# Inverse roots of the scan stage on GpSimd as a power, ScalarE's silus in halves, and two sums around Ln set apart

## What is computed

```python
h = x * rsqrt(mean(x * x, -1) + 1e-5) * norm_scale          # first inverse root, per token
xs, res = split(h @ w_in, 2, -1)
res = silu(res)                                             # the gate
xs = silu(causal_depthwise_conv(xs, conv_w, conv_b))
delta, B, C = split(xs @ w_xproj, [16, 32], -1)
delta = softplus(delta @ w_dt + b_dt)
deltaA = exp(delta[..., None] * -exp(A_log))
deltaBx = (delta * xs)[..., None] * B[:, :, None, :]
ys = scan(h_t = deltaA_t * h_(t-1) + deltaBx_t)             # along the tokens
x2 = layernorm(x + (x + ((sum_n ys * C) + xs * D) * res @ w_out))   # eps 1e-5
n = x2 * rsqrt(mean(x2 * x2, -1) + 1e-8) * norm_weight      # router and experts read n
# sigmoid router, top 2 of 8 experts, expert FFNs 256 -> 1024 -> 256 with relu,
# a shared FFN of the same size, and a last layer norm over x2 + both
```

## Time and profile before

| | |
|---|---|
| median of 3 runs | 1816.91 us (1810.32 to 1822.06) |
| profiled execution, span | 1813.2 us |
| PE busy | 1512.9 us, 83% |
| DVE busy | 1268.1 us, 70% |
| ACT busy | 947.0 us, 52% |
| POOL busy | 888.3 us, 49% |
| the chain that ended last | PE 49%, DVE 30%, ACT 11%, issue 7%, DMA 2% |

### The profile page before, as it was taken

One profiled execution on the slowest core, in us unless ns is written; L12 is line 12 of the kernel. 1 busy time (PEld: TensorE's weight loads), 2 busy tenths in 40 slices (PEclk: granted clock), 3 DMA queues, 4 the chain that ended last, 5 costly groups with the idle time before them and its releaser, 6 DMA issues.

```text
span 1813.2 us, 24484 instructions
## 1 busy us (share of the span) xinstructions
PE 1512.9 (83%) x6945; PEld 968.6 (53%) x6946; DVE 1268.1 (70%) x2203; ACT 947.0 (52%) x1802; POOL 888.3 (49%) x412
## 2 busy tenths in 40 slices
PE   7485789887898997898897857896999999999980
PEld 3121225424434533444443513575999999999970
DVE  3488999999999899999999999622333333333327
ACT  4577666668657568557568644221333333333324
POOL 0676776696685786685786794110111111111114
PEclk9698997898897898897898988988999999999995
DMA  5833653452541642632632641555555555555538
GB/s 153 213 88 76 147 121 74 120 144 61 135 130 48 160 115 67 157 109 55 163 99 65 163 122 24 181 175 198 177 184 188 174 178 189 184 174 177 188 114 271
DMA packets 136951, 252.14 MB, mean 139 GB/s; under 512 B 15313, under 2 KB 68418, under 8 KB 136754
## 3 DMA queue, kind: packets, MB, share of 16 engines
q1 hardware_dynamic: 130402, 233.49, 45.8%
q0 software_dynamic: 6480, 17.83, 2.7%
HBM read 205.76 MB, written 45.51 MB: 139 GB/s over the span
## 4 chain that ended last, share of the span: by engine, by line
PE 49%; DVE 30%; ACT 11%; issue 7%; DMA 2%; SPq 1%; POOL 0%; DVEq 0%; ACTq 0%; POOLq 0%
DVE psH L1041 17%; PE psP L1553 14%; PE psH L1542 14%; DVE big L1050 6%; PE psP L1383 5%; PE psP L1372 4%; PE psA L1481 3%; PE psA L1462 2%; PE psP L1446 2%; PE psP L1401 2%; ACT psH L885 2%; ACT L885 1%; PE psA L1472 1%; PE psP L1530 1%; DMA xb<-rows_dram 1%
## 5 line engine op out<-in xcount | busy, mean ns | idle before, releaser
L467 POOL TENSOR_TENSOR big<-big,B 128x2048 f32<-128x2048 f32 x128 | 578.3, 4528 | 216.3 <-PE psA L1481 140.4
L885 ACT ACTIVATE psH<-big,A_q 128x512 f32<-128x512 f32 x512 | 352.1, 691 | 181.7 <-DVE big L1050 173.3
L1041 DVE TENSOR_TENSOR_SCAN psH<-psH,big 128x512 f32<-128x512 f32 x256 | 312.2, 1220 | 57.3 <-ACT psH L885 37.9
L1050 DVE TENSOR_TENSOR big<-psH,C 128x512 f32<-128x512 f32 x512 | 345.7, 675 | 0.0
L1041 DVE TENSOR_TENSOR_SCAN psH<-psH,carry,big 128x512 f32<-128x512 f32 x256 | 328.4, 1283 | 17.0 <-ACT psH L885 17.0
L508 POOL DMA_INDIRECT con_dram<-eo,dest x71 | 67.8, 955 | 481.2 <-ACT eo L945 473.3
L1481 PE MATMUL psA<-big,gsum 128*32 128x512 f32 x1024 | 236.9, 674 | 64.8 <-DVE big L1050 64.6
L1542 PEld LDWEIGHTS psH<-nTb,ew_s 128*128 128x128 f32 x2272 | 266.1, 193 | 3.6
L1542 PE MATMUL psH<-nTb,ew_s 128*128 128x128 f32 x2272 | 266.3, 276 | 0.0
L1553 PE MATMUL psP<-big,hT 128*128 x1136 | 258.7, 381 | 1.0 <-DVE eb L1291 0.7
L1553 PEld LDWEIGHTS psP<-big,hT 128*128 128x128 f32 x1136 | 211.4, 191 | 27.9 <-issue 1.8
(11 more groups left out here) (180 smaller groups left out, 1593.0 us busy)
## 6 DMA issues: line engine op xcount, KB each, us to landing
ew_s<-in_L_ffn_ew_dram SPq DMA_DIRECT2D x71, 1024.0 KB, 4.9
big<-ud_dram SPq DMA_DIRECT2D x128, 512.0 KB, 8.5
ud_dram<-ud SPq DMA_DIRECT2D x32, 512.0 KB, 2.6
xb<-rows_dram SPq DMA_DIRECT2D x71, 130.0 KB, 2.1
B<-bc_dram SPq DMA_DIRECT2D x128, 64.0 KB, 5.4
C<-bc_dram SPq DMA_DIRECT2D x128, 64.0 KB, 8.5
big<-in_L_ffn_ew_dram SPq DMA_DIRECT2D x8, 1024.0 KB, 12.0
big<-con_dram SPq DMA_DIRECT2D x16, 512.0 KB, 8.8
```

What stands on the lines that cost most here:

```text
L467: nc.gpsimd.tensor_tensor(X[:, Q % NX], rep[:, g % 2, 1], B4[:, f:f + 1, :].broadcast_to([P, NR, TC]), ALU.mult).then_inc(bx_ready, 1)
L885: nc.scalar.activation(psH[:, r, :], rep[:, g % 2, 0, r, :], ACT.Exp, scale=A_q[:, c, r, f:f + 1]).then_inc(dA_ready, 1)
L1041: nc.vector.tensor_tensor_scan(psH[:, r, :], psH[:, r, :], X[:, Q % NX, r, :], start, ALU.mult, ALU.add).then_inc(scan_done, 1)
L1050: nc.vector.tensor_tensor(X[:, Q % NX, r, :], psH[:, r, :], C4[:, f, :], ALU.mult).then_inc(hc_ready, 1)
```

## The change

- The inverse roots are made by POOL as a power with exponent −0.5: two instructions at the start (of 4 and 28 columns) for the first norm, and for each tile a function `roots` of five small instructions behind its `input_step` of step 7 (the last tile's at the end of the stage). ACT's Sqrt and DVE's reciprocals, `inverses` and `biases` are gone. DVE's `add_rows` waits for POOL's result.
- `silu_xs` and `silu_gate` are cut in halves of 1024 columns: xs at (6, 3) and (8, 1) for the next tile, the gate at (3, 2) and (12, 1) of its own tile.
- Of the softplus, `dt_exp` moves from (2, 0) to (1, 3) and from (11, 0) to (10, 3), and 1 + x is made ahead of Ln, at (2, 0) and (11, 0). The subtraction of 1 behind it moves from (11, 3) to (11, 2).
- `read_rows` moves from (2, 0) and (2, 1) to (2, 2) and (3, 0), and one `read_in` from (6, 3) to (7, 0).
- In the start, Exp of A_log is taken earlier.

ACT loads a table 64 times before and 96 times after.

```diff
@@ POOL
+            def roots(k):
+
+                pool.wait_ge(v_ready, k + 1)
+                link.done(nc.gpsimd.tensor_tensor(spread[:, 2], spread[:, 0],
+                                                  less_half[:, 0:2 * NSUB].rearrange("p (a s) -> p a s", a=2),
+                                                  ALU.pow)).wait()
+                link.done(nc.gpsimd.tensor_tensor(nbias[:, 0], mv[:, :, 0], spread[:, 2, 0], ALU.mult))
+                link.done(nc.gpsimd.tensor_tensor(spread[:, 1, 0], spread[:, 0, 0], spread[:, 2, 0], ALU.mult)).wait()
+                nc.gpsimd.tensor_scalar(nbias[:, 0], nbias[:, 0], -1.0, None, ALU.mult).then_inc(nb_ready, 1)
+                nc.gpsimd.tensor_tensor(nbias[:, 1], spread[:, 1, 0], spread[:, 2, 1], ALU.mult).then_inc(n1_ready, 1)
...
+            nc.gpsimd.memset(less_half[:], -0.5).then_inc(s_half, 1)
+            pool.wait_ge(s_half, 1)
+            pool.wait_ge(s_ms, 1)
+            nc.gpsimd.tensor_tensor(rstd1[:, 0:NSUB], rstd1[:, 0:NSUB], less_half[:, 0:NSUB],
+                                    ALU.pow).then_inc(s_rstd, 1)
...
+                    if k >= 1 and q == 7:
+                        roots(k - 1)
...
                     nc.gpsimd.memset(zero[:], 0.0).then_inc(s_base, 1)
+                    roots(NT - 1)
@@ ACT
-            act.wait_ge(s_ms, 1)
-            nc.scalar.activation(rstd1[:, 0:NSUB], rstd1[:, 0:NSUB], ACT.Sqrt).then_inc(s_root, 1)
...
-            def silu_xs(k):
-                evacuated(act, k, ("C", CH - 2), ("C", CH - 1))
-                nc.scalar.activation(xs[:, k % 2], xs[:, k % 2], ACT.Silu).then_inc(xs_ready, 1)
...
+            def silu_xs(k, h):
+                evacuated(act, k, ("C", 2 * h), ("C", 2 * h + 1))
+                part = xs[:, k % 2, 2 * h:2 * h + 2]
+                nc.scalar.activation(part, part, ACT.Silu).then_inc(xs_ready, 1)
...
-                         (2, 0): [(read_rows, 1, 0), (dt_exp, 0, 1)], (2, 1): [(read_rows, 1, 1), (dt_ln, 0, 1)],
-                         (2, 2): [(dt_one_plus, 0, 1)], (2, 3): [(dt_less_one, 0, 1)],
+                         (1, 3): [(dt_exp, 0, 1)], (2, 0): [(dt_one_plus, 0, 1)],
+                         (2, 1): [(dt_ln, 0, 1)], (2, 2): [(read_rows, 1, 0)], (2, 3): [(dt_less_one, 0, 1)],
+                         (3, 0): [(read_rows, 1, 1)], (3, 2): [(silu_gate, 0, 0)],
...
-                         (6, 1): [(read_conv, 1, 1)], (6, 2): [(read_in, 1, 3)], (6, 3): [(read_in, 1, 6)],
...
-                         (8, 0): [(read_conv, 1, 3)], (8, 1): [(root, -1), (silu_xs, 1), (silu_gate, 1)],
+                         (6, 1): [(read_conv, 1, 1)], (6, 2): [(read_in, 1, 3)], (6, 3): [(silu_xs, 1, 0)],
+                         (7, 0): [(read_in, 1, 6)], (7, 1): [(read_conv, 1, 2)], (7, 2): [(read_in, 1, 7)],
+                         (8, 0): [(read_conv, 1, 3)], (8, 1): [(silu_xs, 1, 1)],
...
+                         (12, 0): [(relu_up, -1, 1)], (12, 1): [(silu_gate, 0, 1)], (13, 0): [(relu_up, -1, 2)], (13, 2): [(relu_up, -1, 3)],
@@ DVE
-            def inverses(k):
-                dve.wait_ge(sq_ready, k + 1)
-                link.done(nc.vector.reciprocal(spread[:, 2], spread[:, 1]))
...
             def add_rows(k, h, i):
                 s = 2 * h + i
                 dve.wait_ge(o_done, k * UPS + (h + 1) * PER_HALF)
-                link.wait()
+                dve.wait_ge(n1_ready, k + 1)
...
-                         (8, 0): [(inverses, -1), (biases, -1)],
```

More of the change, by code:

```diff
@@ L797, in dt_ln @@
                     after(act, ud_out[j], 16 * (2 * k + h))
+                nc.scalar.activation(ud[:, :, 0], spe[:], ACT.Copy, bias=1.0).then_inc(sp_act, 1)
+            def dt_ln(k, h):
                 nc.scalar.activation(ud[:, :, 1], spe[:], ACT.Ln, bias=1.0).then_inc(sp_act, 1)
[L800 to L801 removed]
             def dt_less_one(k, h):
[L804 removed]
+                act.wait_ge(sp_act, 6 * (2 * k + h) + 4)
                 nc.scalar.activation(ud[:, :, 0], ud[:, :, 0], ACT.Copy, bias=-1.0).then_inc(sp_act, 1)
@@ L809, in dt_in @@
                 dt_relu(k, c)
-            def root(k):
-                act.wait_ge(v_ready, k + 1)
-                nc.scalar.activation(spread[:, 1], spread[:, 0], ACT.Sqrt).then_inc(sq_ready, 1)
             def normalize(k, i):
@@ L889, in _ @@
                 read_rows(0, d)
+            act.wait_ge(s_A, 16 * NG)
+            nc.scalar.activation(A_q[:], A_q[:], ACT.Exp).then_inc(s_neg, 1)
             read_in(0, 0)
@@ L896, in _ @@
                 evacuated(act, 0, ("C", c))
-                nc.scalar.activation(xs[:, 0, c], xs[:, 0, c], ACT.Silu).then_inc(s_xs0 if c < CH - 1 else xs_ready, 1)
-            act.wait_ge(s_A, 16 * NG)
-            nc.scalar.activation(A_q[:], A_q[:], ACT.Exp).then_inc(s_root, 1)
+                nc.scalar.activation(xs[:, 0, c], xs[:, 0, c], ACT.Silu).then_inc(s_xs0 if c % 2 == 0 else xs_ready, 1)
             read_proj(0)
@@ L913, in _ @@
             nc.scalar.activation(ud[:, 1, 0], ud[:, 1, 0], ACT.Copy, bias=-1.0).then_inc(sp_act, 1)
-            act.wait_ge(s_ms, 2)
-            nc.scalar.activation(rstd1[:, NSUB:], rstd1[:, NSUB:], ACT.Sqrt).then_inc(s_root, 1)
             act.wait_ge(rwT_full, 1)
@@ L1027, in _ @@
             dve.wait_ge(s_u0, 3)
-            dve.wait_ge(xs_ready, 1)
+            dve.wait_ge(s_xs0, 1)
             nc.vector.tensor_tensor(ud[:, 0, 1], ud[:, 0, 0], xs[:, 0, 0], ALU.mult).then_inc(u_ready, 1)
-            dve.wait_ge(s_root, 3)
-            nc.vector.reciprocal(later, later).then_inc(s_rstd, 1)
             def scan(k, q, r):
```

56 lines of the change are left out of this document (26 added, 30 removed).

## The result

The changed kernel takes 1862.99 us in the median of 4 runs (1859.27 to 1867.14), against 1818.82 for the kernel before; the ratio is 1.024, with a 95% interval of 1.0205 to 1.0274. It is slower by 44 us. The forecast was slower at 1850, with a range of 1815 to 1868. The profiled execution spans 1857.5 us, 44.3 more than before.

The account below looks back on a forecast made before the run. The scan stage was taken as bound by DVE's work plus its waits. The terms, −19 + 17 + 8 + 12 + 15 + 0 = +33 us on 1813.2, gave 1846, or 1850 as a median; range 1815 to 1868.

Parts of the forecast that it names:

- A: Step 8: the root leaves ACT and DVE and the silus are halved, so the decay ends earlier; −19 us.
- B: Steps 2 and 3: late T bank reads delay PE's output product, so DVE waits at its residual; +17 us.
- C: Step 12: the gate's second half comes between two decays; +2.0 us in even tiles, +0.7 in odd, +8 in all.
- D: Step 4: one of DVE's small variance instructions falls into a POOL multiplication of 4.5 us; +12 us (0 to 17).
- E: Step 14: DVE's chain of eight can wait for POOL's first two next-tile multiplications; +15 us, 27 at most.
- F: The ends: a 1.28 us load before the first scan, tile 0 −2, tile 7 and tail +1; sum 0.
- G: POOL's power at step 7: taken as 0.5 us, with 10.8 us of room covering all five instructions.
- Rival 1: Port waits between DVE and POOL don't deepen, D and E about 0: 1820 to 1823 us; chance 0.25.
- Rival 2: POOL's multiplications miss the chain at step 14, whose waits go, −12 us: 1811 as a median; chance 0.08.
- Rival 3: The power is dear, above 2 us per instruction, or long at the start: 1870 us and above; chance 0.05.
- rival 4: Something unseen follows table loads; 1885 us if each of 32 added loads costs twice its row; chance 0.02.

## Why the prediction was right, and where its steps were off

- **What bounds the kernel.** The scan stage's DVE chain: all of the 44 us is found between its scans and, with 1.0, ahead of the first.
- **A** held: −19.8 for −19. At step 8 of tile 2 DVE now waits 1.46 us where it waited 2.70, and three instructions are gone. The roots' share of it is half, 9.3 us, by the run with the roots alone. Its split was off: 3.1 to 3.5 in even tiles for 2.8 (2.9 in the sum), 3.2 to 3.3 in odd ones for 3.6. Besides, step 6 is 0.4 longer in even tiles.
- **B** had the right place and cause and half the size: +32.2 for +17. The step that was wrong is the term "PE's next product takes 3.62": it was taken from a row in which PE had been busy ahead of it. With PE idle it takes 6.2 to 6.6, which is 16.3 of the 32 (the run that keeps PE busy). The other half, 15.9, is 2.7 a tile for the 2.8 forecast; with the reads back 3.4 of it stay, which no run explains. "Right or wrong" was to be seen in a wait at L1068 of 2 to 3 us; it is 5.0 to 5.5, and 2.5 to 2.6 with PE kept busy.
- **C** held: +2.1 in even tiles, +0.6 to 0.8 in odd ones, for +2.0 and +0.7.
- **D** was right in kind and a little too large: +8.9 for +12. L1102 takes 2.3 to 3.7 us in these tiles, and L1105 (the L1087 of the earlier trace rows) 0.17 instead of 1.25. The rule ahead of the terms, that any small DVE instruction waits for POOL, was too wide: in the kernel before, the reciprocal just ahead of L1096 goes through in 0.18 us at 402.90, inside the multiplication that POOL began at 400.27.
- **E** was too small: +23.1 for +15 (27 was the bound). The chain meets both multiplications in five of the six tiles and neither in tile 3, where it even gains 0.5. The discount for scattered phases was too large, since nearly every tile came to lie on the bad side of the half microsecond that decides. That this is by POOL coming earlier and DVE later, as E argues, no run separates.
- **F**: the start cost 1.0 us for a forecast 1.3, and tile 0 gave 3.5 for 2.
- **G**: the power takes 1667 ns for 8 columns, not 0.5, and stays hidden in the 10.8 us of room.
- Not in the sum: −6.7 at steps 0 and 1, where waits for ACT's decays shrink. Much the same waits went, by 1.1 to 1.7 us each, in the kernel before with PE kept busy. That it is the clock in the changed kernel too is not shown: over the 10 us ahead of tile 4 the clock is 1.00 for 0.57 before, but ahead of tile 6, where step 0 gains the same 1.7, it is 0.67 for 0.74.

Taken together, B and E were short by 23 us, D and the missing term too high by 10, and the forecast came out 13 low. That it lies so near is in part luck with these errors' signs. The range's upper end fits 1850 with D and E at full (17 more); the "+24" written beside it doesn't follow from the terms.

Rival 1 (port waits don't deepen) is out: D and E measure 32 us. Rival 2 is what the routing chain's move brings about, and there it pays 36 us in the kernel before, three times what its price of 12 said: the held instructions are 15 of them, and what follows at the start of the next tile was not counted. Rival 3 and rival 4 are out: all five of POOL's instructions fit in the room, and in the changed kernel's scan stage what follows a table load starts 0.01 us behind its end, in all 89 of them.

## What to carry to other kernels

A read that frees a PSUM bank has to be priced by what its bank's next product delays, not by its own 0.67 us; and a product that will start behind a new idle stretch of PE, by rows behind such a stretch, since the same 16 products took 3.7 or 6.4 us here. Small VectorE instructions with operands in SBUF belong where GpSimd has nothing in flight by dependency, for instance where it waits for their result: moving eight of them by six places gave 36 us with no work saved, 15 of them in the steps of the chain itself and 17 at the start of the next tile, where PE had been at its lower clock. Where an edit shifts the phase between two such engines, look at each step's time as well as at the total, for one place can give or take 8 us a tile.
